# Local attention scores of a two-branch attention kernel: from 64x128 to 64x64 TensorE tiles

## The reference

```python
bq = q.reshape(b, h, w, WINDOW, d) * QK_SCALE
bk, bv = (look_around(bk), look_around(bv))     # block before, own block
sim = jnp.einsum('bhwid,bhwjd->bhwij', bq, bk)
mask = (i < j) | (i > j + WINDOW) | (j == -1)   # j == -1: no block before the first
sim = jnp.where(mask, -jnp.finfo(sim.dtype).max, sim)
attn = jax.nn.softmax(sim, axis=-1)
out = jnp.einsum('bhwij,bhwjd->bhwid', attn, bv)
```

## Time and profile before

| | |
|---|---|
| median of 3 runs | 3054.31 us (3051.53 to 3061.63) |
| the profiled execution: span, first to last instruction | 3052.9 us |
| its own time | not listed apart; the runs lie at 3051.53, 3054.31 and 3061.63 us |
| PE busy | 2932.4 us |
| DVE busy | 1987.4 us |
| ACT busy | 1704.3 us |
| POOL busy | 1019.2 us |

### The profile page before, as it was taken

How to read it: one execution, slowest core, us unless ns; L and a number is a source line. 1 busy time by engine, 2 the same in 40 slices (tenths; PEclk the granted TensorE clock), 3 DMA queues, 4 the chain that set the end, 5 groups by cost and what they waited for, 6 DMA issues and landing times.

```text
span 3052.9 us, 86127 instructions
## 1 busy us (share of the span) xinstructions
PE 2932.4 (96%) x33792; PEld 2004.3 (66%) x33792; DVE 1987.4 (65%) x6942; ACT 1704.3 (56%) x3094; POOL 1019.2 (33%) x1002
## 2 busy tenths in 40 slices
PE   6999999999999999999999999999999999999997
PEld 4666666676666666666666766666667676666764
DVE  5567676666767566676767666676675766666653
ACT  4455464655555565555556655566565655655552
POOL 5134250424324052352414324152250423423230
PEclk9999999999999999999999999999999999999998
DMA  3000000000000000000000000000000000000000
GB/s 102 2 5 2 10 4 2 12 2 12 2 4 10 2 12 2 9 5 2 12 2 9 5 9 5 2 9 5 8 5 2 12 2 8 5 2 9 2 8 5
DMA packets 41783, 25.03 MB, mean 8 GB/s; under 512 B 13058, under 2 KB 40620, under 8 KB 41388
## 3 DMA queue, kind: packets, MB, share of 16 engines
q1 hardware_dynamic: 41388, 19.52, 2.3%
HBM read 14.96 MB, written 4.19 MB: 6 GB/s over the span
## 4 chain that ended last, share of the span: by engine, by line
PE 83%; DVE 7%; ACT 4%; issue 4%; POOL 2%; DMA 0%; POOLq 0%; DVEq 0%; ACTq 0%
PE bank L1139 10%; PE bank L1182 9%; PE bank L1168 7%; PE bank L1056 7%; PE bank L1223 6%; PE bank L1195 4%; PE bank L1239 4%; PE bank L1208 3%; PE bank L1228 3%; PE bank L1049 3%; PE bank L1261 3%; PE bank L1266 3%; PE bank L1050 3%; PE bank L1051 3%; PE bank L1271 2%
## 5 line engine op out<-in xcount | busy, mean ns | idle before, releaser
L910 DVE CUSTOM_DVE_ANT_0 bank<-bank,future 128x128 f32<-128x128 f32 (+3 forms) x1024 | 467.3, 527 | 68.8 <-PE bank L1098 68.2
L925 DVE CUSTOM_DVE_ANT_0 bank<-bank,band 128x192 f32<-128x192 f32 x1024 | 331.0, 394 | 226.1 <-PE bank L1116 225.7
L714 POOL TENSOR_TENSOR rnorm<-ssc,minus_half 128x8 f32<-128x8 f32 x256 | 426.8, 1667 | 21.3
L780 ACT ACTIVATE probs<-bank 128x512 f32<-128x512 f32 (+1 forms) x768 | 346.0, 532 | 143.7 <-PE bank L1148 143.1
L712 POOL TENSOR_SCALAR ssc<-ss 128x8 f32<-128x8 f32 x256 | 99.7, 390 | 934.4 <-DVE ss L970 930.4
L1139 PE MATMUL bank<-Qa,Ka 64*128 64x512 f32 (+3 forms) x2048 | 391.3, 465 | 8.0 <-ACT lprobs L787 4.4
L1182 PEld LDWEIGHTS bank<-Va,probs 128*64 128x64 f32 x10240 | 312.4, 138 | 47.3 <-issue 38.3
L1182 PE MATMUL bank<-Va,probs 128*64 128x65 f32 x10240 | 332.6, 223 | 0.0
L963 DVE TENSOR_TENSOR scratch<-bank,rope_t 128x512 f32<-128x512 f32 x256 | 176.2, 688 | 230.0 <-ACT scratch L807 207.9
L807 ACT ACTIVATE scratch<-bank 128x512 f32<-128x512 f32 x256 | 153.8, 601 | 259.9 <-PE bank L1223 167.5
L787 ACT ACTIVATE lprobs<-bank 128x512 f32<-128x512 f32 x256 | 139.0, 595 | 283.0 <-PE bank L1170 282.9
(11 more groups left out here) (164 smaller groups left out, 6496.5 us busy)
## 6 DMA issues: line engine op xcount, KB each, us to landing
x_res<-in_L_attn_x SPq DMA_DIRECT2D x16, 256.0 KB, 2.9
x_rows<-in_L_attn_x SPq DMA_DIRECT2D x16, 256.0 KB, 3.2
out<-yT SPq DMA_DIRECT2D x16, 256.0 KB, 2.5
Lqkv<-in_L_ffn_wqkv SPq DMA_DIRECT2D x2, 768.0 KB, 4.8
rope_t<-in_rope SPq DMA_DIRECT2D x8, 128.0 KB, 4.7
Kf<-in_L_attn_W_qkv SPq DMA_DIRECT2D x1, 768.0 KB, 7.4
Qf<-in_L_attn_W_qkv SPq DMA_DIRECT2D x1, 768.0 KB, 9.0
Lw<-in_L_ffn_w SPq DMA_DIRECT2D x2, 341.0 KB
```

The lines of the kernel that those rows point to most:

```text
L714: g.tensor_tensor(rnorm[s][:, :], ssc[:, :], minus_half[:, :], ALU.pow).then_inc(rnorm_ready.sem, 1)
L780: psum.raise_read(a.activation(probs[j][:, at:at + n], psum.bank(i, task, (u, j))[:, 0:n], ACT.Exp, scale=float(HEAD) ** -0.5), i, task, ( ...
L910: ins = v.tensor_tensor_reduce(psum.bank(i, task, (u, j))[:, at:at + n], psum.bank(i, task, (u, j))[:, at:at + n], future[:, SEQ - n:SEQ], ...
L925: ins = v.tensor_tensor_reduce(psum.bank(i, task, (u, j))[:, k * BAND:(k + 1) * BAND], psum.bank(i, task, (u, j))[:, k * BAND:(k + 1) * BAND],
```

## The change

The scores of `f_st` are now made in 64x64 tiles. Each block of 64 keys is loaded once and streamed by both query blocks that see it: its own and the next. Even key blocks go to output partitions 0 to 63, odd ones to 64 to 127. So for an even query block its own block is in the lower half and the block before in the upper half, and for an odd query block it is the other way round. All masks follow that: each is now four products of 64x64 tiles (two heads, two halves) with a stride over every second block. The values of the turned blocks are called `V_turned` and stay in their partitions. The key pad and two mask tensors go. In the planner's tables `f_st` gets 1.35 us and a tile shape of its own, "quarters", so the order of tasks can come out another way.

```diff
-    "f_st": both([1.5]) + [("act", 0.62, (0,), (), (b,)) for b in range(2)],
+    "f_st": both([1.35]) + [("act", 0.62, (0,), (), (b,)) for b in range(2)],
...
-TILING = {"a_max": "rows", "a_st": "rows", "f_max": "rows", "f_st": "rows", "a_pv": "columns", "f_pv": "columns"}
+TILING = {"a_max": "rows", "a_st": "rows", "f_max": "rows", "f_st": "quarters", "a_pv": "columns", "f_pv": "columns"}
...
-        ahead = sb("ahead", [P, SEQ], BF16)
+        passed = sb("passed", [P, BLOCKS // 2, BLOCK], BF16)
         no_key = sb("no_key", [P, BLOCK], BF16)
-        masked_last = sb("masked_last", [P, P], BF16)
...
-        K_padded = [sb(f"Kf{l}", [P, BLOCK + LPAIRS * SEQ]) for l in range(DEPTH)]
-        Kf = [part[:, BLOCK:].rearrange("p (c n) -> p c n", c=LPAIRS) for part in K_padded]
+        Kf = [sb(f"Kf{l}", [P, LPAIRS, SEQ]) for l in range(DEPTH)]
...
-                sp.dma_start(ahead[rows, :], below[0:BLOCK, :]).then_inc(halved, 16)
+            sp.dma_start(passed[BLOCK:P, :, :], passed[0:BLOCK, :, :]).then_inc(halved, 16)
...
-                const(g.memset(below, 0.0))
-                select(below.rearrange("p (b n) -> p b n", n=BLOCK), ALU.is_ge, MASK_BAND, 0, [[0, BLOCKS], [1, BLOCK]], -1)
+                const(g.memset(passed[:, :, :], 0.0))
+                select(passed[:, :, :], ALU.is_ge, MASK_BAND, 0, [[0, BLOCKS // 2], [-1, BLOCK]], 1)
                 const(g.memset(no_key[:, :], MASK_BAND))
-                const(g.memset(masked_last[:, :], 0.0))
-                for part in HALF:
-                    select(masked_last[:, 0:HEAD], ALU.not_equal, MASK_ROW, -part.start, [[-1, HEAD]], 1)
-                    select(masked_last[:, :], ALU.not_equal, -1.0, 1 - part.stop, [[0, P]], 1)
-                for part in K_padded:
-                    const(g.memset(part[:, 0:BLOCK], 0.0))
...
-                    a.activation(V_shifted[l][HALF[1], t, :, 0:HEAD], bank[HALF[0]], ACT.Copy)
+                    a.activation(V_turned[l][HALF[0], t, :, 0:HEAD], bank[HALF[0]], ACT.Copy)
                     if t + 1 < TILES:
-                        a.activation(V_shifted[l][HALF[0], t + 1, :, 0:HEAD], bank[HALF[1]], ACT.Copy)
+                        a.activation(V_turned[l][HALF[1], t + 1, :, 0:HEAD], bank[HALF[1]], ACT.Copy)
...
-                                    negf[p % 2][:, t, (j + 1) * HEAD - 1:(j + 1) * HEAD])
+                                    negf[p % 2][:, t, j * HEAD:j * HEAD + 1])
...
+                    four = [(h, j) for h in range(2) for j in range(2)]
+                    queries = [[bank[j][part, :].rearrange("p (b two n) -> p b two n", two=2, n=BLOCK) for part in HALF] for j in range(2)]
+                    shift = negfT[p % 2][:, :].rearrange("p (b two n) -> p b two n", two=2, n=BLOCK)
                     for j in range(2):
-                        mm(bank[j][:, :], row_of[HALF[j], 1, :], ahead[HALF[j], :], start=True, stop=False)
-                    for j in range(2):
-                        mm(bank[j][:, 0:BLOCK], row_of[HALF[j], 0, :], no_key[HALF[j], :], start=False, stop=False)
-                    for b in range(BLOCKS):
-                        keys = slice(p * SEQ + b * BLOCK, p * SEQ + (b + 2) * BLOCK)
-                        queries = slice(b * BLOCK, (b + 1) * BLOCK)
-                        for j in range(2):
-                            mm(bank[j][:, queries], K_padded[l][HALF[j], keys], Qf[l][HALF[j], p, queries],
-                               start=False, stop=False)
-                    last = [mm(bank[j][:, :], masked_last[HALF[j], :], negfT[p % 2][HALF[j], :], start=False, stop=True)
-                            for j in range(2)]
+                        mm(queries[j][1][:, 0, 0, :], row_of[HALF[j], 0, 0:BLOCK], no_key[HALF[j], :], start=True, stop=False)
+                    for b in range(0, BLOCKS, 2):
+                        for h, j in four:
+                            own = slice((b + h) * BLOCK, (b + h + 1) * BLOCK)
+                            seen = slice(own.start, min(own.stop + BLOCK, SEQ))
+                            mm(bank[j][HALF[h], seen], Kf[l][HALF[j], p, own], Qf[l][HALF[j], p, seen], start=(b + h == 0), stop=False)
+                    for h, j in four:
+                        mm(queries[j][h][:, h:, 1 - h, :], row_of[HALF[j], 0, 0:BLOCK], passed[HALF[j], h:, :], start=False, stop=False)
+                    for h, j in four:
+                        mm(queries[j][h][:, :, 1 - h, :], minus_first[HALF[j], 0:BLOCK], shift[HALF[j], :, 1 - h, :], start=False, stop=False)
+                    last = [mm(queries[j][h][:, :, h, :], masked_first[HALF[j], 0:BLOCK], shift[HALF[j], :, h, :], start=False, stop=True)
+                            for h, j in four][2:]
...
-                        V = (Vf if b % 2 else V_shifted)[l]
+                        V = (Vf if b % 2 else V_turned)[l]
...
-CONSTS = 54
-HALVED = 16 * 10
+CONSTS = 47
+HALVED = 16 * 9
```

More of the change, by code:

```diff
@@ L479, in prenorm_attention_and_local_transformer @@
         Qf = [sb(f"Qf{l}", [P, LPAIRS, SEQ]) for l in range(DEPTH)]
-        K_padded = [sb(f"Kf{l}", [P, BLOCK + LPAIRS * SEQ]) for l in range(DEPTH)]
-        Kf = [part[:, BLOCK:].rearrange("p (c n) -> p c n", c=LPAIRS) for part in K_padded]
+        Kf = [sb(f"Kf{l}", [P, LPAIRS, SEQ]) for l in range(DEPTH)]
         Vf = [sb(f"Vf{l}", [P, TILES, LHEADS, HEAD + 1]) for l in range(DEPTH)]
-        V_shifted = [sb(f"V_shifted{l}", [P, TILES, LHEADS, HEAD + 1]) for l in range(DEPTH)]
+        V_turned = [sb(f"V_turned{l}", [P, TILES, LHEADS, HEAD + 1]) for l in range(DEPTH)]
         negf = [sb(f"negf{b}", [P, TILES, P], BF16) for b in range(2)]
@@ L507, in prenorm_attention_and_local_transformer @@
         GLU = sb("GLU", [P, len(HID_CHUNKS), SEQ])
-        below = GLU[:, 0, :].bitcast(BF16)[:, 0:SEQ]
         banks = [ctx.enter_context(nc.psum_tensor(f"bank{k}", [P, 512], F32)) for k in range(8)]
@@ L661, in make_rest @@
                 select(band[:, :, :], ALU.is_ge, MASK_BAND, WINDOW, [[0, 2], [-1, BAND]], 1)
-                const(g.memset(below, 0.0))
-                select(below.rearrange("p (b n) -> p b n", n=BLOCK), ALU.is_ge, MASK_BAND, 0, [[0, BLOCKS], [1, BLOCK]], -1)
+                const(g.memset(passed[:, :, :], 0.0))
+                select(passed[:, :, :], ALU.is_ge, MASK_BAND, 0, [[0, BLOCKS // 2], [-1, BLOCK]], 1)
                 const(g.memset(no_key[:, :], MASK_BAND))
-                const(g.memset(masked_last[:, :], 0.0))
-                for part in HALF:
-                    select(masked_last[:, 0:HEAD], ALU.not_equal, MASK_ROW, -part.start, [[-1, HEAD]], 1)
-                    select(masked_last[:, :], ALU.not_equal, -1.0, 1 - part.stop, [[0, P]], 1)
-                for part in K_padded:
-                    const(g.memset(part[:, 0:BLOCK], 0.0))
-                for part in V_shifted:
+                for part in V_turned:
                     const(g.memset(part[:, 0, :, :], 0.0))
@@ L691, in make_rest @@
                     const(g.memset(negf[b][:, :, :], 0.0))
-                    select(negf[b][:, :, :].rearrange("p t (j r) -> p (t j) r", j=2), ALU.is_ge, MASK_BAND, 0, [[0, 2 * TILES], [1, HEAD]], -1)
+                    select(negf[b][:, :, :].rearrange("p t (j r) -> p (t j) r", j=2), ALU.is_ge, MASK_BAND, 0, [[0, 2 * TILES], [-1, HEAD]], 1)
                 assert made[0] == CONSTS, made[0]
```

## The result

The changed kernel takes 2987.01 us (median of 4 runs, 2985.46 to 2993.63) against 3052.92 us for the kernel before (median of 4 runs, one more than the forecast had, whose three gave 3054.31), a ratio of 0.9781 (95% interval 0.9766 to 0.9796). It is faster by 66 us. The forecast was 2939 us, 114 us faster, with a range from 2916 to 2978. So the direction was right and the size was not: 48 us of the forecast gain did not arrive, and the time lies outside the range.

A forecast was written before the change was run, and what follows sets the result against it. PE's instruction stream bounds the kernel: 3052.9 us span - 129.3 (shorter steps) + 10.5 (shape changes) + 6 (waits) - 2.7 (start) = 2937.4, so 2939 us as run time; range 2916 to 2978.

The forecast's parts named there:

- What bounds the kernel, and the scores: PE's instruction stream is the time; local score step falls from 2.28 to 1.27 us, saving 129.3 us over 128 steps.
- Rival A: Local score step: only two of the four tiles run together, step 2.48 us, 3094 us in all; chance 5%.
- rival B: Local score step: four bf16 groups each wait 0.06 us for slow weight loads, +31 us, 2970 us; chance 10%.
- Changes of tile shape: PE entering and leaving f_st: 105 more shape changes at 0.10 us each, +10.5 us.
- Waits uncovered: PE's waits for other engines, which get 1.01 us less per f_st: +6 us, bounds 0 and +39.
- the +6: Microseconds added for PE waits on other engines that the shorter f_st no longer covers.
- Rival C: Other engines are late for PE: +39 us of waits instead of +6, 2972 us; chance 8%.
- The limit of 100: PE idle time from 100 us to the end: above 100 us would show that the other engines are late.
- The step that failed: Planner's task order: may gather f_st steps another way under the new tile shape; bounds 0 and +12 us.
- Rival E: Whole kernel: step is shorter but the new order costs as much in waits, about 3050 us; chance 2%.
- Slow bf16 loads: Mask and maximum products in f_st: column tiling excludes the fast weight load; expected hidden under the 0.11 us stream.
- Start: POOL's chain of constants ahead of PE's first large product: shorter by 2.7 us, bounds 0 and -3.

The follow-up runs named there:

- the tight order: Changed kernel with a wider, stricter planner search (80 courses kept, other due times, spread 0.25, weight 0.1): 2874.40 us, ratio 0.9414 to the kernel before.

## Why the prediction was wrong, point by point

**What bounds the kernel, and the scores.** Right. PE's stream is the time, and the step went from 2.28 to 1.26 us, forecast 1.27. Rival A (two of four tiles at once, 2.48 us) and rival B (bf16 loads exposed) did not happen. The trace had rows side by side and columns side by side and no step with both; to expect the two together was right. In the old order PE is busy for 2814.6 us, where the prediction had set 2815 as a sign of being right; in the changed kernel it is 2830.9.

**Changes of tile shape.** The price was right at 0.10 us, the number was not: the list has 1313 in place of 1170, 143 more instead of 105. That is 4 us. In the old order there are 1275, exactly the 105 more.

**Waits uncovered.** For what I described, the other engines having 1.01 us less per step, the +6 is borne out. In the old order 3053.3 - 2935.4 = 117.9 us were saved; 128 x 1.02 less 10.5 and with 2.4 at the start would be 122.5, which leaves 4 to 5 us for all waits. In the tight order the same sum leaves about 2. Rival C's +39 did not happen. Its sign did, with 128.9 us of idle time from 100 us to the end, but the sign didn't belong to C alone: with the same code in the old order it is 96.4. The limit of 100 was also too close to the 94.5 of the kernel before to tell much.

**The step that failed** is the sentence "The planner is told of the new form and may gather steps another way; bounds 0 and +12". It priced the new order by its changes of shape alone, which left it 1.5 us above the 10.5 already counted. Everything else it kept as in the old order: the idle time, the end, and the clock at the end, for which the sum has no term. The order costs 52 us more than the old one with the same code (2987.0 against 2935.4), about 48 of them apart from its 38 further changes of shape. In the profiled executions that is 49.0 us: 32.7 of idle time, 4 for the changes of shape, by estimate 6 for the clock, and the rest in waits too short to show.

Rival E had the mechanism, "the new order costs as much in waits", but only as an all-or-nothing case of 3050 us with 2%, and so the range ended at 2978 and held nothing between. The planner searches with 40 courses kept, and a small change of its table can lead it elsewhere: an entry moved by 0.15 us and one new shape gave 58 us more by its own count. Nothing in the profile of before gives the size. The program does: with its own table each, the planner ends at 3023 us before the change and at 3073 after it, later and not earlier, and that could have been worked out ahead of any run. The forecast of 2939 us is near what the code does in the old order, 2935.

**Slow bf16 loads** were weighed rightly: they take 108 ns in the new tiles, and the stream hides it.

**Start.** 2.4 us for 2.7.

## What to carry to other kernels

When a change touches a table that a planner reads, there are two changes, and each should be timed alone: new code in the old order and old code in the new order cost two runs and tell them apart. They need not agree to the microsecond: the order cost 52 us with the new code and 63 with the old. Run the planner with both tables first and compare where it says that it ends. Before pricing an edit, ask what a pass waits for: here a 64-column stream stood behind a 128-column float32 load, and a load no longer than the stream, in four tiles at once, gave nearly all of the gain; the number of loads saved gave a tenth. And look at the last stretch of a pipeline separately: when the independent work is spent, the dependent rest pays twice, in idle time (20.0 us here) and in a clock that falls to half in part of it (some 6 us).

## What the runs showed that I had not expected

Tiles of the 64x64 form do not keep step with each other: in the timeline of the changed kernel a later group starts in one tile (L1164 at 1508.08) before an earlier one in another (L1162 at 1508.09). In this step the tiles with shorter streams made nobody wait.

PE accepts one pass per 18 ns on average over a step of 74 passes, each with its own weight load.

The planner's count of its own end, though its cost for `f_st` was 1.5 us before the change, where the step took 2.28, ranks the orders well: 58 us between two orders by its table were 52 measured, 126 were 113, and 45 with the old code were 37.
